# A decoder layer: norm and context turned by transfers of 16-bit planes, loop starts of VectorE and POOL moved, the keys' scaling on ScalarE

## What is computed

```python
x = x + mamba(layernorm(x))              # W_in, causal conv of 4 taps, SSD of 64 tokens, 8 heads of 64, gated RMS norm, W_out
x = x + cross_attention(layernorm(x), ctx, mask)   # 16 query heads, 4 key/value heads of 128, RMS norm of q and k
x = x + ffn(layernorm(x))                # ternary weights, activations quantised to 8 bits, 256 -> 1024 -> 256

k = rmsnorm((ctx @ Wk + bk).reshape(b, se, NKV, HD), kn_w)
v = (ctx @ Wv + bv).reshape(b, se, NKV, HD)
zxbcdt = layernorm(x) @ W_in
```

## Time and profile before

| | |
|---|---|
| median of 3 runs | 1210.87 us (1210.43 to 1211.52) |
| the profiled execution | 1213.46 us |
| its span, first to last instruction | 1211.3 us |
| mean granted TensorE clock in it | 0.982 |
| PE, DVE (VectorE), ACT (ScalarE), POOL busy | 95%, 83%, 61%, 80% |

### The profile page before, as it was taken

How to read it: one execution, slowest core, us unless ns; L and a number is a source line. 1 busy time by engine, 2 the same in 40 slices (tenths; PEclk the granted TensorE clock), 3 DMA queues, 4 the chain that set the end, 5 groups by cost and what they waited for, 6 DMA issues and landing times.

```text
span 1211.3 us, 34542 instructions
## 1 busy us (share of the span) xinstructions
PE 1153.1 (95%) x11579; PEld 990.5 (82%) x11579; DVE 1000.5 (83%) x2509; ACT 735.4 (61%) x1879; POOL 963.5 (80%) x1546
## 2 busy tenths in 40 slices
PE   4889999999999999999999999999999999999974
PEld 3778888889888888988888898888889888888753
DVE  4767888888889888888988888898888889888556
ACT  4685566665556676555667655566755556675532
POOL 4798878889888888888888888888888888878651
PEclk8899999999999999999999999999999999999987
DMA  8210000000000000000000000000000000001000
GB/s 299 78 54 11 24 19 15 26 26 26 22 26 13 17 26 26 26 22 26 13 17 26 26 26 22 26 8 22 26 26 26 22 26 4 26 24 23 14 10 22
DMA packets 63400, 36.78 MB, mean 30 GB/s; under 512 B 40448, under 2 KB 61696, under 8 KB 63104
## 3 DMA queue, kind: packets, MB, share of 16 engines
q1 hardware_dynamic: 60432, 36.24, 10.4%
q10 hardware_dynamic: 2928, 0.03, 0.1%
HBM read 23.93 MB, written 4.19 MB: 23 GB/s over the span
## 4 chain that ended last, share of the span: by engine, by line
PE 49%; DVE 17%; POOL 15%; issue 14%; ACT 3%; POOLq 1%; DVEq 1%; DMA 0%; SPq 0%; ACTq 0%
PE bank L1689 10%; PE bank L1580 4%; PE bank L1581 4%; PE bank L1582 4%; DVE xc L1120 4%; PE bank L1749 3%; PE bank L1608 3%; PE bank L1662 3%; PE bank L1771 3%; PE bank L1617 3%; POOL pr L483 2%; PE bank L1803 2%; PE bank L1825 1%; PE bank L1808 1%; DVE mx L1238 1%
## 5 line engine op out<-in xcount | busy, mean ns | idle before, releaser
L1689 PE MATMUL bank<-xcT,wq 128*128 128x128 f32 x2048 | 236.1, 276 | 1.3 <-ACT xcT L783 1.3
L1689 PEld LDWEIGHTS bank<-xcT,wq 128*128 128x128 f32 x2048 | 231.1, 192 | 5.6 <-issue 1.6
L1120 DVE SCALAR_TENSOR_TENSOR xc<-bank,cw,xc 128x124 f32<-128x124 f32 (+2 forms) x576 | 163.8, 340 | 8.3 <-ACT xc L753 3.5
L471 POOL TENSOR_TENSOR rq<-rq,minus_half 128x16 f32<-128x16 f32 x32 | 93.8, 2933 | 88.8 <-DVE rq L1221 88.8
L1580 PE MATMUL bank<-wo_hi,o_hi 128*128 128x256 f32 x512 | 149.9, 293 | 1.1 <-DVE o_lo L1209 1.1
L1581 PE MATMUL bank<-wo_lo,o_hi 128*128 128x256 f32 x512 | 144.6, 282 | 0.0
L1582 PE MATMUL bank<-wo_hi,o_lo 128*128 128x256 f32 x512 | 144.5, 282 | 0.0
L802 ACT ACTIVATE qT<-bank,bqT 128x128 f32<-128x128 f32 x384 | 109.3, 371 | 51.9 <-PE bank L1689 51.8
L1580 PEld LDWEIGHTS bank<-wo_hi,o_hi 128*128 128x128 f32 x512 | 97.6, 191 | 1.4 <-DVE o_lo L1209 1.4
L1581 PEld LDWEIGHTS bank<-wo_lo,o_hi 128*128 128x128 f32 x512 | 97.4, 190 | 0.1
L1582 PEld LDWEIGHTS bank<-wo_hi,o_lo 128*128 128x128 f32 x512 | 97.3, 190 | 0.0
(11 more groups left out here) (235 smaller groups left out, 3402.5 us busy)
## 6 DMA issues: line engine op xcount, KB each, us to landing
x_in<-in_x SPq DMA_DIRECT2D x32, 128.0 KB, 2.1
c_in<-in_ctx SPq DMA_DIRECT2D x32, 128.0 KB, 2.0
x_m<-in_x SPq DMA_DIRECT2D x32, 128.0 KB, 2.2
out<-x SPq DMA_DIRECT2D x32, 128.0 KB, 1.7
wq<-in_L_xattn_Wq SPq DMA_DIRECT2D x1, 2048.0 KB, 14.2
stage<-in_L_xattn_Wo SPq DMA_DIRECT2D x2, 1024.0 KB, 8.0
w_in<-in_L_attn_W_in SPq DMA_DIRECT2D x1, 1024.0 KB, 6.2
qT<-in_L_ffn_w_gate SPq DMA_DIRECT2D x1, 1024.0 KB, 11.3
```

Of the source, the lines that this page charges most:

```text
L471: g.tensor_tensor(rq[:, 1, :], rq[:, 0, :], minus_half[:, :], ALU.pow).then_inc(s["x_rq"].sem, 1)
L1120: last = v.scalar_tensor_tensor(out=o, in0=src, scalar=cw[:, j, TAPS - 1 - back:TAPS - back], in1=o, op0=ALU.mult, op1=ALU.add)
L1689: last = mm(x_Qbank[g][:, (n % 4) * P:(n % 4 + 1) * P], wq[:, c, n * HD:(n + 1) * HD], xcT[:, c, :], start=(c == 0), stop=(c == DC - 1))
```

## The change

1. The norm m_xn (from tile 4 on) and the context c_in (from tile 2 on) are no longer turned by PE. ScalarE splits the 32-bit values in a plane of high and one of low 16-bit halves (`m_split_halves`, `c_split_halves`), SP issues a transposing transfer of the 128x512 halves (`turn_m`, `turn_c`), and ScalarE joins the turned halves to 32-bit values in m_xnT and xcT (`m_join_halves`, `c_join_halves`). The planes lie in m_sq and in q2. `m_transpose` and `m_xnT_copy` leave the body, `x_transpose` and `x_T_copy` keep the x half alone. `m_join_halves(mn)` runs in the body after the one of `m_split_halves`, right behind `m_tap_x`; the context is split and joined in one body. `load_ctx` and VectorE's `m_norm` wait for the splits in place of PE's turns.
2. The multiplication of the keys goes from POOL to ScalarE (`x_khat` there, four instructions with a scale for each token).
3. VectorE: `x_scale` 0 and 1 of the next body and `f_stats` stand, in this order, at the loop's end; the loop starts at `x_max`. POOL: its body is cut in `first` and `second`, and the loop starts at `second`, at `x_rms`.

```diff
+        m_halves = m_sq[:, 0:XCH // 2, :].rearrange("p a b -> p (a b)").bitcast(U16)
+        m_halvesT = m_sq[:, XCH // 2:, :].rearrange("p a b -> p (a b)").bitcast(U16).rearrange("p (g n) -> p g n", g=2 * DC)
...
+            def turn_m(t):
+                count(sp, s["m_planes"], t - M_TURN + 1)
...
+                sp.dma_start_transpose(m_halvesT, m_halves).then_inc(s["m_turned"].sem, 16)
...
                 if not isinstance(i, int) or i > 3:
                     store(i - 4)
+                if not isinstance(i, int) or M_TURN <= i + 2 < TILES:
+                    turn_m(i + 2)
+                if not isinstance(i, int) or C_TURN <= i < TILES:
+                    turn_c(i)
                 if not isinstance(i, int) or 2 < i < TILES + 2:
                     turn_h(i - 3)
...
-                after(pool, s["x_rk"], t + 1)
-                g.tensor_tensor(kb[:], kb[:], bcast(kss[:, 2, :].unsqueeze(2), [P, NKV, HD]),
-                                ALU.mult).then_inc(s["x_kh"].sem, 1)
...
+            first(*tiles(5))
+            with pool.Fori(5, TILES - 3) as i:
+                second(i + 2, i + 1, i, i - 1, i - 2, i - 3, i - 4)
+                first(i + 3, i + 2, i + 1, i, i - 1, i - 2, i - 3)
+            second(*tiles(TILES - 3))
...
+            def m_split_halves(t):
+                after(act, s["m_xn"], t + 1)
+                count(act, s["m_turned"], (t - M_TURN) * 16)
+                sc.copy(m_halves.rearrange("p (g n) -> p g n", g=2),
+                        m_xn[:].bitcast(U16).rearrange("p (n g) -> p g n", g=2)).then_inc(s["m_planes"].sem, 1)
+
+            def m_join_halves(t):
+                count(act, s["m_turned"], (t - M_TURN + 1) * 16)
+                after(act, s["m_X1"], t)
+                sc.copy(m_xnT[:].rearrange("p c n -> p (c n)").bitcast(U16).rearrange("p (n g) -> p g n", g=2),
+                        m_halvesT.rearrange("p (g c) n -> p g (c n)", g=2)).then_inc(s["m_xnT"].sem, 1)
...
+                chunks = 2 * DC if isinstance(t, int) and t < C_TURN else DC
+                sc.copy(xcT[:, 0:chunks, :], X2[:, 0:chunks * P].rearrange("p (c n) -> p c n", c=chunks)).then_inc(s["x_TT"].sem, 1)
...
+            def x_khat(t):
+                after(act, s["x_rk"], t + 1)
+                for n in range(NKV):
+                    last = sc.activation(kb[:, n, :], kb[:, n, :], ACT.Copy, scale=kss[:, 2, n:n + 1])
+                last.then_inc(s["x_kh"].sem, 1)
...
+            def begin(i):
+                x_scale(i - 2, 0)
+                x_scale(i - 2, 1)
+                f_stats(i - 3)
...
+            begin(5)
             with dve.Fori(5, TILES - 2) as i:
                 body(i + 2, i + 1, i, i - 1, i - 2, i - 3, i - 4)
+                begin(i + 1)
...
                     x_attend(xb, 0, xa)
-                if mn is not None:
-                    m_transpose(mn)
                 if xb is not None:
                     x_attend(xb, 1, xa)
```

More of the change, by code:

```diff
@@ L9 @@
 BF16 = mybir.dt.bfloat16
+U16 = mybir.dt.uint16
 F32R = mybir.dt.float32r
@@ L291, in load_ctx @@
             def load_ctx(t):
-                after(sp, s["x_T"], t)
+                if isinstance(t, int) and t <= C_TURN:
+                    after(sp, s["x_T"], t)
+                else:
+                    count(sp, s["c_planes"], t - C_TURN)
                 sp.sem_inc(s["sp_waited"].sem, 1)
@@ L626, in tail, with first @@
                 f_rms(x)
-            def body(ms, mn, m, xa, xb, f, fb, extra=None):
+            def first(ms, mn, m, xa, xb, f, fb):
                 if xb is not None:
@@ L652, in body, with second @@
                     x_o_low(xb, 1)
+            def second(ms, mn, m, xa, xb, f, fb):
                 if xa is not None:
@@ L671, in _ @@
             fill()
[L672 to L675, removed]
+            for i in range(3, 5):
+                first(*tiles(i))
+                second(*tiles(i))
+            first(*tiles(5))
[3 more added lines that the diff above has]
+            second(*tiles(TILES - 3))
             for i in range(TILES - 2, TILES + 1):
-                body(*tiles(i))
+                first(*tiles(i))
+                second(*tiles(i))
             tail(TILES - 3, TILES - 2, TILES - 1)
@@ L989, in body @@
                     m_tap_x(m)
+                if mn is not None:
+                    m_join_halves(mn)
                 if xa is not None:
@@ L1050, in body @@
                     x_kT_copy(xa)
+                if m is not None:
+                    c_join_halves(m)
+                if xa is not None:
                     x_keep(xa)
@@ L1090, in m_norm @@
             def m_norm(t):
-                after(dve, s["m_T"], t)
+                if isinstance(t, int) and t <= M_TURN:
+                    after(dve, s["m_T"], t)
+                else:
+                    count(dve, s["m_planes"], t - M_TURN)
                 normalise(t, x_in[:], m_mv, m_xn, s["m_rstd"], s["m_xn"])
@@ L1564, in _ @@
             dve.wait_ge(s["w_small"].sem, 16 * W_SMALL)
+            begin(3)
             body(*tiles(3), extra=3)
+            begin(4)
             body(*tiles(4))
+            begin(5)
             with dve.Fori(5, TILES - 2) as i:
                 body(i + 2, i + 1, i, i - 1, i - 2, i - 3, i - 4)
-            for i in range(TILES - 2, TILES + 1):
+                begin(i + 1)
+            for i in range(TILES - 2, TILES):
                 body(*tiles(i))
+                begin(i + 1)
+            body(*tiles(TILES))
             tail(TILES - 3, TILES - 2, TILES - 1)
@@ L1670, in x_transpose @@
                 after(pe, s["x_xn"], t + 1)
-                count(pe, s["c_loaded"], t * 16 + 16)
                 after(pe, s["x_kT"], t)
                 for c in range(DC):
-                    nc.tensor.transpose(X2[:, c * P:(c + 1) * P], x_xn[:, c * P:(c + 1) * P], ident[:])
-                for c in range(DC):
-                    last = nc.tensor.transpose(X2[:, (DC + c) * P:(DC + c + 1) * P], c_in[:, c * P:(c + 1) * P], ident[:])
+                    last = nc.tensor.transpose(X2[:, c * P:(c + 1) * P], x_xn[:, c * P:(c + 1) * P], ident[:])
+                if isinstance(t, int) and t < C_TURN:
+                    count(pe, s["c_loaded"], t * 16 + 16)
+                    for c in range(DC):
+                        last = nc.tensor.transpose(X2[:, (DC + c) * P:(DC + c + 1) * P], c_in[:, c * P:(c + 1) * P], ident[:])
                 last.then_inc(s["x_T"].sem, 1)
```

49 lines of the change are left out of this document (40 added, 9 removed).

## The result

The changed kernel takes **1197.76 us** (median of 4, 1197.11 to 1197.89). Beside it on the same chip the kernel before took 1211.19 (median of 4, 1210.43 to 1215.31). The ratio is 0.9879 with a 95% interval of 0.9864 to 0.9894: 1.2% faster. The forecast was 1202.8 with a range of 1193 to 1209.5. The sign holds, and the time lies in that range, which was kept wide for the rivals. It lies outside the forecast's own range of 1199 to 1207. The gain is 13.4 where 8.1 was forecast, and most of this document is about why.

A forecast was written before the change was run, and what follows sets the result against it. The prediction took PE, held by VectorE at the product, as the bound; 26 bodies of 0.29 us plus the ends gave -8.1, so 1210.87 - 8.1 = 1202.8 us, with 1199 to 1207 its own range and 1193 to 1209.5 over all cases.

The forecast's parts named there:

- PE held by VectorE at the product: At the second up-projection PE waits for VectorE's product of the first half, held back by at least 0.29 us a body.
- longer than 0.6 us: Sign of a right prediction: PE still waits at the product after the change, for longer than 0.6 us.
- The two paths: PE's work then ScalarE's decay, and VectorE's scaling, POOL's mask, VectorE's convolution and sums, meet at mw with nearly one length.
- the meeting point: Start of VectorE's mw: decay side allows 0.29 earlier, VectorE's side 0.38; the later wins, so 0.29 us a body.
- VectorE's loop start: x_scale moved to the loop's end brings scaling and mask 0.4 to 1.0 us earlier, of which only 0.4 is needed.
- The norm worth nothing: Removing PE's m_transpose (0.44 us) between the attention's halves gains nothing on the path; it only lengthens PE's wait at the product.
- POOL's multiplication: Taking the keys' multiplication (1.04 us) off POOL brings the mask earlier, inside the 0.4 to 1.0 already counted.
- ScalarE: Added plane copies (0.58 us assumed, 0.96 upper end) and key scaling (1.14) fit in idle time: cost zero.
- slower rival of dear copies: ScalarE's plane copies of every second 16-bit element cost far more; at 2.0 us a copy, 1226; chance 0.05.
- The transfers: Two added transposing transfers in SP's queue, at worst 4.4 us each, have the context there by 604.8, in time: cost zero.
- The first rival: POOL's shift separates it from VectorE's mw and f_xn, which get shorter: 1188, or 1194 with f_xn alone; chance 0.15.
- The sum: Loop bodies 7.5, body 3 0.3, body 30 0.4, bodies 31 and 32 0.4 gained, 0.5 lost before the loop: -8.1 us.

The follow-up runs named there:

- e11: The changed kernel with four of eight m_project_bc products moved on PE to between second gate projection and second up-projection: 1191.69 us, ratio 0.9814 to the kernel before.
- e5: The changed kernel with the context turned by PE again, without its splits, transfer and join: 1210.31 us, ratio 0.9984 to the kernel before.
- e6: The changed kernel with two added PE transposes of x_xn in the context's place, read by nothing: 1205.47 us, ratio 0.9931 to the kernel before.
- e1: The changed kernel with VectorE's scaling and f_stats back at their old places: 1210.4 us, ratio 0.9986 to the kernel before.
- e8: The changed kernel with the keys' multiplication back on POOL: 1202.14 us, ratio 0.9915 to the kernel before.
- e12: The changed kernel with POOL's norm variance steps moved behind its x_o_low and VectorE's m_norm behind f_weight: 1189.19 us, ratio 0.9797 to the kernel before.
- e3: The changed kernel with VectorE's and POOL's loop starts both back, leaving transfers and the keys' scaling on ScalarE: 1211.6 us, ratio 0.9991 to the kernel before.
- e7: The changed kernel with the norm turned by PE again, context still by transfer: 1198.98 us, ratio 0.989 to the kernel before.
- e9: The changed kernel with VectorE's m_norm moved to behind f_weight: 1198.23 us, ratio 0.9875 to the kernel before.
- e2: The changed kernel with POOL's loop start alone back ahead of the mask: 1199.51 us, ratio 0.9895 to the kernel before.

## Why the prediction was right in sign and short in size

**What bounds the kernel, PE held by VectorE at the product.** Right: the wait stands in the change as it stood, and filling it with PE's own work (e11) gives back 0.29 a body. That is near the "at least 0.29" read from body 30 of the kernel before; since two kernels are compared, the equality proves nothing. The sign "longer than 0.6 us" failed: the longest wait is 0.6 still, because the product came earlier by 0.54 and not by 0.29, nearly as much as PE's own work shrank.

**The two paths.** The step that failed is the meeting point: "the decay side allows mw at 582.49 - 0.21, which is 0.29 before 582.57; VectorE's side allows 0.38. The later wins". Two things are wrong in it. The smaller is a term: the decay side gained 0.34 and not 0.21, because the queries wait for x_T_copy too, whose shorter half the prediction counted for the tap alone (e5 and e6: 0.35 with it, 0.21 without). mw began 0.08 after the decay, as foretold, but at S + 14.66, not at 14.80; by the prediction's own rule that is 0.43 a body. The larger is the rule: mw's start is not what counts. Four runs show it. The decay came 0.34 earlier in e1 and the period stayed; the decay stayed in e8 and the period grew by 0.09; in e5 decay and tap moved by different amounts, and the period took the tap's; in e12 the decay stayed, mw began where it did, and 0.41 went. What goes with the period in every run of e1 to e8 is the convolution's start: the period is that start plus 28.63 to 28.68. Behind the convolution VectorE's sums feed POOL, which then works through x_prob, the norm's variance, m_skip, x_split and x_o_low, and VectorE's mw and m_gate end 0.54 to 0.56 after POOL's xd and x_o_low, from whatever point they began (e12's mw alone is free of it). So the row of work that sets the product runs convolution, POOL, m_gate, and not decay, mw. e8 moves its first member, e12 its middle.

**Where the paths do meet** is the convolution. Its start is the later of x_max's end less 0.08 or 0.09 and the tap's end plus 0.03 or 0.04, in every row of the table. Before, x_max was the later by 0.12 (6.80 against 6.68). The change moved x_max's side by 0.77 and the tap's by 0.44, to 6.25. That is 0.55, and 0.52 of it reached the period. The prediction had both of these limits: "I need only 0.4 of it, for the next limit is the convolution", and for the tap 0.21 for the transposes and 0.17 for the shorter copy. These came out at 0.22 (e6) and 0.22 (e5 less e6), which is 0.06 of the miss. The 0.12 of x_max was overlooked, because 574.13 lay only 0.15 ahead of the convolution's start and passed for its releaser.

**VectorE's loop start.** Right in mechanism: the mask moved by 0.76, inside the 0.4 to 1.0, the scaling by 1.09, a little beyond. Without it the rest is worth 0.01 (e3); the prediction said so for the case that VectorE did not come earlier.

**The norm worth nothing.** Right, 0.02 (e7), but for another reason than the one given: in the kernel before VectorE was the later of the two at the skip step only by 0.07 (S + 17.80 against 17.73, the end of PE's m_mix), and what hides the norm in the change is that m_gate ends with POOL.

**POOL's multiplication.** Said to lie inside the mask's surplus. It is worth 0.09 a body (e8), because the mask then misses the tap by 0.11. The room was taken as 0.4 to 1.0 where only 0.20 was left.

**ScalarE.** The splits take 0.61 and 0.62 for the assumed 0.58, the join 0.79, under the upper end of 0.96; the scaling of the keys 1.27 for 1.14. The join is hidden (e7), and q_bias(0) waits 0.22 still. For the splits and the scaling no run isolates the cost; the keys' scaling ends at 590.89, and PE turns the keys at S + 31.53, 591.75. The slower rival of dear copies is out.

**The transfers.** They land in 2.4 (3.8 at worst for the context's). The Trainium skill (VectorE: DVE Perf Modes, Rules for kernel authors) would have kept the transposes on TensorE. Here the two that stood ahead of the tap cost 0.42 a body there, with their copy (e5). As transfers they hold nothing that the trace shows: ScalarE has no idle time ahead of either join (L779, L791) that a landing ended.

**The first rival, VectorE faster through POOL's shift.** Right that this dependence is what decides, wrong in how. It was priced as a shorter mw and f_xn if the two engines came apart. The two did not come apart in the change; both moved together by 0.54 to 0.55, and the dependence carried POOL's gain to VectorE. The case it priced is e12, where mw is 0.10 and f_xn 0.35 shorter. So that the time fell inside the range over all cases, whose lower end was this rival's smaller price, is luck: the rival as priced did not happen. The Trainium skill (SBUF — State Buffer, Who interferes with whom) says that a VectorE instruction with two inputs in SBUF contends with a POOL instruction that reads SBUF, and calls the ports that they share an exclusive lock. The trace agrees: mw and m_gate have two such inputs, and the tail of 0.55 behind POOL's end is the same whether the instruction had begun 0.25 before that end (mw in the change) or 0.81 (m_gate in e9). Why the tail is shorter than mw's free 0.69 no run shows.

**The sum.** The loop gave 13.3 for 7.5, and body 3 0.26 for 0.3 (36.16 for 36.42). Body 30 gave nothing (35.22 for 35.14) where 0.4 was forecast: f_down waits there for h_q's transfer, which landed in 4.4 for a median of 2.7.

```profile
1053.88 1.05 PE L1918 MATMUL bank<-wdT,h_q 128*128 128x256 bf16 x8 [0.53 <-DMA h_q<-h_q]
```

This belongs to the execution and not to the change alone: e9 waits in the same place (landing 4.3, body 35.19), and e2, whose bodies are equal, does not (3.3, body 34.53). What delays the landing is open. Body 31 took 33.65 for 33.26, body 32 30.76 for 32.51. The stretch before body 3 came 1.0 earlier (105.00 for 105.98) where 0.5 of loss was forecast; with the keys on POOL it was 105.92. But the first scores of all start between 67.4 and 69.7 in these kernels, in no order that follows the edits, so no cause is claimed for the ends; none of them was tested alone.

## What to carry to other kernels

Where two engines hold each other, an instruction's start says little: read its end against the end of the other engine's instruction, and follow the chain through that engine. When a start has two releasers within 0.15 us, treat both as limits, and add up what the change does to each; a change may need both halves at once, as this one, where the halves are worth 0.01 and 0.10 and the whole 0.52. And if PE waits for one product and nothing else, look first for work of its own that can be put under the wait: that took one moved group of four products, and gave 0.29 a body.

## What the hardware showed that was not expected

- VectorE's instructions of two SBUF inputs (mw and m_gate, both 128x512 f32) end 0.54 to 0.56 us after the two-input POOL instruction (xd, x_o_low) that ran when they began, in all runs but for e12's mw, which began when xd was done and took its free 0.69. Starting 0.18 earlier made m_gate 0.17 longer (e9), 0.23 later made it 0.22 shorter (e7).
- It goes both ways: POOL's cast of c_hi takes 0.85 beside mw, and 0.39 in e12, where VectorE works on single columns meanwhile. There c_lo, which began 0.13 after mw, takes 1.14, for 0.73 in the change.
- ScalarE copies 512 16-bit elements a partition in 0.61 when it reads every second one and writes densely, and in 0.79 the other way round.
- A transposing transfer of 512 16-bit columns takes SP 1.2 and lands in 2.4, for 1.26 and 2.7 with 1024 columns: half the data takes nearly the same. Single ones land later, at worst 3.8 (the context's) and 4.6 (h_q's).
- VectorE's loop start costs 0.41 of idle time when nothing covers it (e1; body 30 of e1, behind the loop, has none there), and POOL's nothing here, since it falls in a wait (e2).
